# Fifteen loops over sequences, written out before, become counted loops in the engines' programs

## The chip, the cores and the metric

The kernel runs on one core of a Trainium2 chip. The metric is the device time of one execution in microseconds (us). Each of the core's five engines runs a program of its own: TensorE (PE in the profile, and PEld for its weight loads), VectorE (DVE), ScalarE (ACT), GpSimd (POOL) and SyncE (SP, which here only issues DMAs). The engines meet through semaphores alone: an instruction adds to one when it ends, another instruction waits until one has reached a number.

## The reference

The input is x, 4 sequences of 1024 tokens by 256 features. It is normalised, and the result is x plus two branches:

```
xn = layernorm(x)
out = x + attention(xn) + ffn(xn)
attention: rms norm, q/k/v for 16 heads of 64, window of 64, softmax, gate by sigmoid, W_out
ffn:       2 layers, each: shift tokens; q/k/v for 8 heads of 64; l2 norm and rotary; window of 128,
           softmax, wo, add; shift, layernorm, w1 (682 x 2), a * gelu(g), w2, add
```

All is float32. Products of activations and weights are formed as three products of a high and a low part, to keep float32's accuracy.

## The kernel before

The kernel has two phases, one after the other. `attention_phase` (L170) goes over 4 sequences and splits, on the way, the layers' weights into high and low parts. `layers_phase` (L903) goes over 8 sequences: the 4 of layer 0 and then the 4 of layer 1. A sequence is handled as two halves of 512 tokens.

What is done for a sequence stands in a table of steps, `A_ORDER` (L133) for the attention and `ORDER` (L888), taken twice, for the layers: ("scores", 0), ("softmax", 0), ("weigh", 0) and so on. In each engine's program a function `iteration(it, steps, ...)` walks through the same table and emits this engine's part of each step: TensorE the products of a "scores" (L613, L1358), VectorE the masking and the row maximum (L840, L1608), ScalarE the exponentials (L748, L1517), GpSimd the scaling of "weigh" (L522, L1236), TensorE the "transpose" (L621, L1366) and the "values" (L636, L1381). In the layers there follow the products `up` (L1406), ScalarE's Gelu of them (L1533, which needs another table than the exponentials, so that an ACT_TABLE_LOAD stands ahead of it), and `down` (L1420). The order of each engine is the order of the table.

The numbers that are waited for come from the class `Count`. One count says how many times a semaphore is raised in one iteration, and `upto` works out the value:

```
if it is None:
    return self.credit + self.unit * (n + 1)
return it * (self.unit * self.each) + (self.credit + self.unit * (self.before + n + 1))
```

Here `it` is the number of the sequence. Where it is a number of Python, the value is a constant in the instruction. The last iteration of a phase leaves out the steps that prepare a next sequence (`last`), and stands apart, as does iteration 3 of the layers for SP, PE and ACT, in which weights or tables of the other layer are loaded.

Every engine has such loops over `it`: one of 3 in the attention; in the layers one of 3 (4 for DVE and POOL) and one of 3. In the kernel before they are loops of Python: the program of an engine holds each iteration's instructions one after another.

An instruction of a compute engine holds one wait of its own. A wait before that becomes an EVENT_SEMAPHORE, an instruction of the engine's sequencer, which stands still at it. Where two waits stand before an instruction, the build decides which of the two goes into it.

TensorE's results go to three banks in turn; `take_bank` (L532, L1270) waits until the one who reads the bank of three results ago is through (semaphores `emptied` and `copied`), and the step itself waits for its operand: the transposes L621 and L1366 for `normalized`, which GpSimd raises.

## Time and profile before

| | |
|---|---|
| device time, median of 3 runs | 2094.42 us (2092.75 to 2094.42) |
| device time of the profiled execution | 2094.42 us |
| its span, first to last instruction | 2092.4 us |
| granted TensorE clock, mean | 0.978 of full speed |
| busy PE, PEld, DVE, ACT, POOL | 91%, 75%, 63%, 67%, 46% |
| records of PE, PEld, DVE, ACT, POOL | 15184, 15184, 4117, 3933, 1311 |
| one sequence of the attention | 164.6 us |
| one sequence of the layers | 164.0 us (layer 0), 166.4 us (layer 1) |

### The profile page before, as it was taken

Reading aid. Unit: us, or ns where it says so; the run is one execution under the profiler, and the core shown is the slowest. Engines: PE = TensorE matmul, PEld = TensorE weight load, DVE = VectorE, ACT = ScalarE, POOL = GpSimd, SP = SyncE. Lnnn points to the kernel's source line nnn. Section 1 sums busy time; section 2 is a strip of 40 time slices with the busy share of each in tenths; the row PEclk is TensorE's granted clock in tenths of the full one; section 3 lists DMA queues with packets and bytes.
Section 4 is the critical chain, followed back from the end, with each engine's and each line's share of the span. In section 5 each row is a group of like instructions: output and inputs, shape, how many; then the busy total and the mean of one; then the engine's idle time right before and its main releaser. Section 6 shows DMA issues by size and latency. Waiting matters only on the chain.

```text
span 2092.4 us, 42526 instructions
## 1 busy us (share of the span) xinstructions
PE 1901.2 (91%) x15184; PEld 1576.9 (75%) x15184; DVE 1322.5 (63%) x4117; ACT 1402.3 (67%) x3933; POOL 963.3 (46%) x1311
## 2 busy tenths in 40 slices
PE   5999999999998479999999999996999999999998
PEld 3777787777777358788787787885878878778777
DVE  4543543444443168778777777785777877777765
ACT  4886977878778155856757757665576675675764
POOL 1532442433334055626536547353473663654732
PEclk9999999999999689999999999998999999999999
DMA  3231231322212600110110101304011011010110
GB/s 124 90 95 46 91 105 53 95 69 90 91 51 78 228 31 11 44 44 11 41 36 22 41 11 44 104 6 149 21 44 54 21 44 54 11 52 21 34 33 26
DMA packets 120580, 121.16 MB, mean 58 GB/s; under 512 B 27172, under 2 KB 100916, under 8 KB 120372
## 3 DMA queue, kind: packets, MB, share of 16 engines
q1 hardware_dynamic: 108848, 100.89, 15.1%
q10 hardware_dynamic: 11524, 17.57, 2.4%
q8 instruction: 122, 2.00, 0.4%
q14 instruction: 86, 0.70, 0.1%
HBM read 72.78 MB, written 37.25 MB: 53 GB/s over the span
## 4 chain that ended last, share of the span: by engine, by line
PE 32%; DVE 19%; ACT 9%; POOL 3%; issue 2%; ACTq 2%; DVEq 0%; POOLq 0%
PE f_bank L1283 12%; PE f_scores L1420 4%; PE f_scores L1358 4%; ACT f_prob L1517 4%; DVE f_u L1673 4%; PE f_bank L1366 4%; PE f_bank L1406 4%; DVE f_gu L1670 2%; PE f_o_bank L1381 2%; ACT f_u L1537 2%; PE f_bank L1330 2%; DVE f_x_tok L1656 2%; DVE f_x_tok L1662 1%; POOL f_prob L1236 1%; DVE f_rstd L1649 1%
## 5 line engine op out<-in xcount | busy, mean ns | idle before, releaser
L1236 POOL TENSOR_SCALAR f_prob<-f_prob,f_row_inv 128x256 f32<-128x256 f32 x512 | 264.0, 535 | 343.7 <-DVE f_row_inv L1616 343.7
L522 POOL TENSOR_SCALAR a_prob<-a_prob,a_row_inv,a_gate 128x128 f32<-128x128 f32 x512 | 226.2, 462 | 409.7 <-DVE a_row_inv L849 409.7
L1283 PE MATMUL f_bank<-f_wqkv,f_actT 128*128 128x512 f32 x1152 | 302.8, 407 | 14.9 <-DVE f_actT L1559 14.9
L1406 PE MATMUL f_bank<-f_hT,f_w 128*128 128x256 f32 x2112 | 275.3, 285 | 7.7 <-DVE f_gu L1670 7.7
L1406 PEld LDWEIGHTS f_bank<-f_hT,f_w 128*128 128x128 f32 x2112 | 261.0, 189 | 14.3 <-DVE f_gu L1670 10.8
L1283 PEld LDWEIGHTS f_bank<-f_wqkv,f_actT 128*128 128x128 f32 x1152 | 209.1, 191 | 64.1 <-issue 17.8
L1517 ACT ACTIVATE f_prob<-f_scores,f_neg_max 128x256 f32<-128x256 f32 x512 | 236.3, 489 | 30.2 <-DVE f_neg_max L1608 29.3
L1212 POOL TENSOR_TENSOR f_norm<-f_norm,f_minus_half 128x16 f32<-128x16 f32 x64 | 199.6, 3119 | 47.1 <-DVE f_norm L1568 45.3
L1608 DVE CUSTOM_DVE_ANT_0 f_scores<-f_scores,f_mask 128x256 f32<-128x256 f32 x512 | 199.8, 455 | 15.5 <-PE f_scores L1358 15.4
L1537 ACT ACTIVATE f_u<-f_gu 128x256 fp32r<-128x256 f32 x192 | 80.2, 418 | 181.8 <-DVE f_gu L1670 181.8
L748 ACT ACTIVATE a_prob<-a_scores,a_neg_max 128x128 f32<-128x128 f32 x512 | 179.9, 391 | 29.0 <-DVE a_neg_max L840 28.7
L545 PE MATMUL a_bank<-a_xT,a_wqkv 128*128 128x512 f32 x768 | 192.7, 403 | 0.0
L1218 POOL TENSOR_TENSOR f_qk_tok<-f_qk_tok,f_tables 128x512 f32<-128x512 f32 x128 | 161.6, 1284 | 62.0 <-DVE f_sin_part L1576 62.0
L1673 DVE TENSOR_TENSOR f_u<-f_gu,f_u 128x256 fp32r<-128x256 f32 x192 | 125.7, 654 | 92.9 <-ACT f_u L1537 92.9
L1461 ACT ACTIVATE f_probT<-f_bank 128x512 f32<-128x512 f32 x256 | 146.0, 613 | 55.6 <-PE f_bank L1366 54.3
L1358 PE MATMUL f_scores<-f_kT,f_q 64*128 64x256 f32 x1024 | 149.5, 409 | 32.7 <-ACT f_prob L1517 32.1
L1366 PE MATMUL f_bank<-f_ident,f_prob 128*128 128x128 f32 x1024 | 148.7, 283 | 30.4 <-POOL f_prob L1236 17.5
L545 PEld LDWEIGHTS a_bank<-a_xT,a_wqkv 128*128 128x128 f32 x768 | 143.7, 191 | 36.0 <-issue 2.5
L1420 PE MATMUL f_scores<-f_w,f_u 128*128 128x256 f32 (+1 forms) x1152 | 163.9, 286 | 0.0
L1366 PEld LDWEIGHTS f_bank<-f_ident,f_prob 128*128 128x128 f32 x1024 | 111.6, 143 | 66.2 <-issue 37.9
L1420 PEld LDWEIGHTS f_scores<-f_w,f_u 128*128 128x128 f32 (+1 forms) x1152 | 147.7, 188 | 6.1 <-issue 2.5
L840 DVE CUSTOM_DVE_ANT_0 a_scores<-a_scores,a_mask 128x128 f32<-128x128 f32 x512 | 129.8, 325 | 35.5 <-PE a_scores L613 35.5
(124 smaller groups left out, 3847.3 us busy)
## 6 DMA issues: line engine op xcount, KB each, us to landing
split_weights<-a_hi_lo SPq DMA_DIRECT2D x16, 512.0 KB, 2.8
f_x_next<-states SPq DMA_DIRECT2D x32, 256.0 KB, 3.1
f_tables<-scaled_tables SPq DMA_DIRECT2D x16, 512.0 KB, 6.1
f_x<-states SPq DMA_DIRECT2D x16, 512.0 KB, 5.0
split_weights<-a_hi_lo SPq DMA_DIRECT2D x12, 682.0 KB, 4.1
f_w<-split_weights ACTq DMA_DIRECT2D x4, 1280.0 KB, 13.2
a_x_tok<-in_x SPq DMA_DIRECT2D x8, 512.0 KB, 4.7
states<-a_x_tok SPq DMA_DIRECT2D x8, 512.0 KB, 3.1
```

The source lines that it names most:

```text
L522: last = nc.gpsimd.tensor_scalar(part, part, row_inv[:, a % 2, head, t:t + 1], gate[:, half, t, h:h + 1], ALU.mult, ALU.mult)
L545: last = nc.tensor.matmul(out, lhs(c, a), rhs(c, b), start=(i == 0), stop=(i == len(order) - 1))
L1212: nc.gpsimd.tensor_tensor(n, n, minus_half[:], ALU.pow).then_inc(norm_ready.sem, 1)
L1236: last = nc.gpsimd.tensor_scalar(part, part, row_inv[:, a % 2, head, t:t + 1], 1.0, ALU.mult, ALU.mult)
L1283: last = nc.tensor.matmul(out, lhs(c, a), rhs(c, b), start=(i == 0), stop=(i == len(order) - 1))
L1358: mm = nc.tensor.matmul(scores[a % 2][head][:, t, :], q[rows, pair, col:col + P], kT[rows, pair, col:col + 2 * P], start=True, stop=True)
L1366: last = nc.tensor.transpose(out[:, j * P:(j + 1) * P], prob[:, a % 2, head, j // 2, (j % 2) * P:(j % 2 + 1) * P], ident[:])
L1406: mm = nc.tensor.matmul(out[:, which * PART:(which + 1) * PART], w1[:, wp, c, col:col + P], hT[:, hp, c, columns_of(a // FH)], start=(i == ...
L1420: mm = nc.tensor.matmul(y_banks[a // FH % PARTS][:, t, :], u[0:m, a % (2 * TILES), up, t * P:(t + 1) * P], w2[0:m, wp, j, :], start=(j == ...
L1517: last = nc.scalar.activation(prob[:, a % 2, head, t, :], scores[a % 2][head][:, t, :], ACT.Exp, bias=neg_max[:, a % 2, head, t:t + 1], sc ...
L1608: last = nc.vector.tensor_tensor_reduce(out=sc, in0=sc, in1=mask[:, min(half * TILES + tile + t, 1)], scale=-1.0, scalar=3e38, op0=ALU.add ...
L1673: nc.vector.tensor_tensor(u[0:m, a % (2 * TILES), LO, :], gu[0:m, a % 2, :], u[0:m, a % (2 * TILES), HI, :].bitcast(F32), ALU.subtract).th ...
```

## The change

The fifteen `for it in range(...)` loops become counted loops of the engine (`Fori`), with the same bounds. The loops' bodies, the tables of steps, tiles, transfers and the iterations that stand apart stay as they are. The diff is the same edit in ten places; the attention's five engines have one loop each, the layers' two:

```diff
@@ attention: SP L469, POOL L526, PE L662, ACT L764, DVE L878
-            for it in range(0, BATCH - 1):
+            with pe.Fori(0, BATCH - 1) as it:
                 iteration(it, steps)
             iteration(BATCH - 1, last)
@@ layers: SP L1190, PE L1425, ACT L1539 (the last with two loads between)
-            for it in range(0, BATCH - 1):
+            with pe.Fori(0, BATCH - 1) as it:
                 iteration(it, steps, 0, 0)
             iteration(BATCH - 1, steps, 0, 1)
-            for it in range(BATCH, SEQUENCES - 1):
+            with pe.Fori(BATCH, SEQUENCES - 1) as it:
                 iteration(it, steps, 1, 1)
             iteration(SEQUENCES - 1, last, 1, 1)
@@ layers: POOL L1262, DVE L1681
-            for it in range(0, BATCH):
+            with dve.Fori(0, BATCH) as it:
                 iteration(it, steps, 0)
-            for it in range(BATCH, SEQUENCES - 1):
+            with dve.Fori(BATCH, SEQUENCES - 1) as it:
                 iteration(it, steps, 1)
             iteration(SEQUENCES - 1, last, 1)
```

`it` is now a register. The value that an instruction waits for is worked out by register instructions ahead of it, and at the end of a body stand an addition and a branch back.

At TensorE, in the layers, before, where sequence 0 ends and sequence 1 begins (L1420 is `down`, L1358 "scores", L1290 the transposes of the next tokens):

```order
L1420 MATMUL f_scores<-f_w,f_u 128x256 [waits f_u_ready]
L1420 MATMUL f_scores<-f_w,f_u 128x256 x5
L1358 MATMUL f_scores<-f_kT,f_q 128x256 [waits f_exped,f_copied]
L1358 MATMUL f_scores<-f_kT,f_q 128x256 x3
L1358 MATMUL f_scores<-f_kT,f_q 128x256 [waits f_exped,f_x2_ready]
L1358 MATMUL f_scores<-f_kT,f_q 128x256 x3
L1290 MATMUL f_bank<-f_ident,f_x_next 128x128 [waits f_copied,f_emptied,f_x_loaded]
```

The same place of the changed kernel, first the end of the body:

```order
L1414 REGISTER_ALU
L1420 MATMUL f_scores<-f_w,f_u 128x256 [waits f_u_ready]
L1420 MATMUL f_scores<-f_w,f_u 128x256 x5
L1425 REGISTER_ALU
L1425 COMPARE_AND_BRANCH
```

and then its beginning, to which that branch goes (ISA is an instruction that works out several registers at once):

```order
L1425 ISA
L1353 ISA [waits f_copied]
L1358 MATMUL f_scores<-f_kT,f_q 128x256 [waits f_exped]
L1358 MATMUL f_scores<-f_kT,f_q 128x256 x3
L1351 ISA
L1358 MATMUL f_scores<-f_kT,f_q 128x256 [waits f_exped,f_x2_ready]
L1358 MATMUL f_scores<-f_kT,f_q 128x256 x3
```

A register addition and a branch have come in between `down` and "scores", and behind the branch two instructions that work out registers. Elsewhere in the body a REGISTER_ALU stands ahead of nearly every instruction that waits.

At TensorE, in the same sequence, before, the transposes of the probabilities (L1366):

```order
L1358 MATMUL f_scores<-f_kT,f_q 128x256 [waits f_exped]
L1358 MATMUL f_scores<-f_kT,f_q 128x256 x3
L1366 MATMUL f_bank<-f_ident,f_prob 128x128 [waits f_normalized,f_emptied]
L1366 MATMUL f_bank<-f_ident,f_prob 128x128 x3
L1366 MATMUL f_bank<-f_ident,f_prob 128x128 [waits f_normalized,f_copied]
L1366 MATMUL f_bank<-f_ident,f_prob 128x128 x3
```

The same in the changed kernel's body (an earlier pair of them):

```order
L1366 MATMUL f_bank<-f_ident,f_prob 128x128 x3
L1273 REGISTER_ALU
L1364 REGISTER_ALU [waits f_emptied]
L1366 MATMUL f_bank<-f_ident,f_prob 128x128 [waits f_normalized]
L1366 MATMUL f_bank<-f_ident,f_prob 128x128 x3
L1353 REGISTER_ALU
```

The waits of two-wait instructions have changed places. The names in the first of these fences are those of all waits ahead of a row; in the program a semaphore instruction holds `normalized` and the transpose holds `emptied` or `copied`. In the changed kernel the register instruction holds `emptied` and the transpose holds `normalized`.

At ScalarE, in the layers, before, where the Gelu of a sequence's first half begins:

```order
L1461 ACTIVATE f_v<-f_bank 128x512 [waits f_filled]
L1467 ACTIVATE f_hT<-f_bank 128x2x256 [waits f_filled]
L1533 ACT_TABLE_LOAD [waits f_filled]
L1533 ACTIVATE f_gu<-f_bank,f_rows 128x256 [waits f_rows_loaded]
L1537 ACTIVATE f_u<-f_gu 128x256 [waits f_emptied]
```

and in the changed kernel's body:

```order
L1466 REGISTER_ALU
L1467 ACTIVATE f_hT<-f_bank 128x2x256 [waits f_filled]
L1529 REGISTER_ALU [waits f_rows_loaded]
L1533 ACT_TABLE_LOAD
L1533 ACTIVATE f_gu<-f_bank,f_rows 128x256 [waits f_filled]
L1536 REGISTER_ALU
L1537 ACTIVATE f_u<-f_gu 128x256 [waits f_emptied]
```

`filled` is raised when TensorE has finished the first `up`. The table was loaded behind that wait, and is now loaded ahead of it. Where the Gelu of the second half begins it is the other way round. Before:

```order
L1461 ACTIVATE f_v<-f_bank 128x512 [waits f_filled]
L1467 ACTIVATE f_hT<-f_bank 128x2x256 [waits f_filled]
L1533 ACT_TABLE_LOAD [waits f_u_ready]
L1533 ACTIVATE f_gu<-f_bank,f_rows 128x256 [waits f_filled]
L1537 ACTIVATE f_u<-f_gu 128x256 [waits f_emptied]
```

and in the changed kernel's body:

```order
L1467 ACTIVATE f_hT<-f_bank 128x2x256 [waits f_filled]
L1529 REGISTER_ALU
L1531 REGISTER_ALU [waits f_filled]
L1533 ACT_TABLE_LOAD
L1533 ACTIVATE f_gu<-f_bank,f_rows 128x256 [waits f_u_ready]
L1536 REGISTER_ALU
L1537 ACTIVATE f_u<-f_gu 128x256 [waits f_emptied]
```

Here the table load stood behind a wait for an `up` of the first half and ahead of `filled`, and stands now behind `filled`.

## Rows read from the trace of the kernel before

**Rows 1.** The page, busy time of each engine

```profile
PE 1901.2 (91%) x15184; PEld 1576.9 (75%) x15184; DVE 1322.5 (63%) x4117; ACT 1402.3 (67%) x3933; POOL 963.3 (46%) x1311
```

**Rows 2.** Stretches: us, busy (x) of PE, PEld, DVE, ACT, POOL, PEclk, DMA, GB/s

```profile
207.10:371.70 164.60, 156.75 (x1449) 126.85 (x1448) 74.15 (x371) 128.63 (x413) 62.99 (x134) 0.99 0.25 80
1090.20:1254.20 164.00, 156.42 (x1178) 131.90 (x1177) 125.71 (x328) 109.78 (x285) 85.99 (x94) 1.00 0.10 32
```

**Rows 3.** The page, DMA queues of the programs: packets, MB, share of 16 engines

```profile
q8 instruction: 122, 2.00, 0.4%
q14 instruction: 86, 0.70, 0.1%
```

**Rows 4.** Timeline of PE, an attention sequence's first instructions: start us, us, instruction

```profile
207.14 1.98 PE L613 MATMUL a_scores<-a_kT,a_q 64*64 64x128 f32 x64
```

**Rows 5.** L605 in 204 to 208 us: ns min/median/max, first and last start

```profile
L605 PEldq EVENT_SEMAPHORE  x2: 51/51/51, 205.2 to 207.4; - x2
```

**Rows 6.** Timeline of all engines, end of a layer sequence

```profile
1087.99 2.46 PE L1420 MATMUL f_scores<-f_w,f_u 128*128 128x256 f32 x17
1090.18 0.48 PE L1358 MATMUL f_scores<-f_kT,f_q 64*128 64x256 f32 x1
1091.64 0.43 DVE L1608 CUSTOM_DVE_ANT_0 f_scores<-f_scores,f_mask 128x256 f32<-128x256 f32 x1 [0.34 <-PE f_scores L1358]
1092.55 0.47 ACT L1517 ACTIVATE f_prob<-f_scores,f_neg_max 128x256 f32<-128x256 f32 x1 [1.85 <-DVE f_neg_max L1608]
```

**Rows 7.** L1353 and L1677 in 1080 to 1092 us

```profile
L1353 PEldq EVENT_SEMAPHORE  x2: 51/51/51, 1088.8 to 1089.5; - x2
L1677 DVEq EVENT_SEMAPHORE  x2: 21/21/21, 1088.3 to 1088.4; - x2
```

**Rows 8.** DMA issues: KB each, median us from issue to landing

```profile
f_x_tok<-f_x SPq DMA_DIRECT2D x16, 0.5 KB, 1.7
f_x_tok<-f_x SPq DMA_DIRECT2D x32, 15.0 KB, 2.2
a_kT<-a_k_kept SPq DMA_DIRECT2D x32, 32.0 KB, 2.8
```

**Rows 9.** Sequencer instructions of two lines, whole span

```profile
L1364 PEldq EVENT_SEMAPHORE  x256: 51/51/51, 768.2 to 2049.8; - x128
L907 SPq COMPARE_BRANCH  x1: 33/33/33, 2091.7 to 2091.7; - x1
```

**Rows 10.** Timeline at 235.5 to 236.1 us, a wait held by the sequencer

```profile
235.33 0.46 POOL L522 TENSOR_SCALAR a_prob<-a_prob,a_row_inv,a_gate 128x128 f32<-128x128 f32 x1
235.93 0.41 PE L621 MATMUL a_bank<-a_ident,a_prob 128*128 128x128 f32 x2 [0.92 <-POOL a_prob L522]
```

**Rows 11.** Timeline at 974.0 to 974.4 us, a wait held by the instruction

```profile
973.77 0.48 DVE L1662 SCALAR_TENSOR_TENSOR f_x_tok<-f_x_tok,f_rstd,f_rows 128x256 f32<-128x256 f32 x1
974.30 0.33 PE L1299 MATMUL f_bank<-f_ident,f_x_tok 128*128 128x128 f32 x1 [0.24 <-DVE f_x_tok L1662]
```

**Rows 12.** Waits: us in total, times, longest

```profile
PE f_bank L1366 <- POOL f_prob L1236: 17.5, 45, 0.7
PE f_bank L1366 <- DVE f_actT L1559: 11.3, 14, 0.8
PE a_bank L621 <- POOL a_prob L522: 10.0, 13, 1.1
PE a_bank L621 <- ACT a_v L697: 8.3, 8, 1.8
PE f_bank L1299 <- DVE f_x_tok L1662: 7.1, 16, 4.0
```

**Rows 13.** Timeline of ACT, first Gelu of a first half, then of a second

```profile
815.49 1.28 ACT L1533 ACT_TABLE_LOAD   x1 [3.93 <-PE f_bank L1406]
816.79 0.48 ACT L1533 ACTIVATE f_gu<-f_bank,f_rows 128x256 f32<-128x256 f32 x1
897.47 0.47 ACT L1533 ACTIVATE f_gu<-f_bank,f_rows 128x256 f32<-128x256 f32 x1 [2.58 <-PE f_bank L1406]
```

More of the change, by code:

```diff
@@ L467, in iteration @@
                         sp.dma_start(rows_out[it // HALVES], rows[:]).then_inc(rows_stored.sem, 16)
-            for it in range(0, BATCH - 1):
+            with sp.Fori(0, BATCH - 1) as it:
                 iteration(it, steps)
@@ L524, in iteration @@
                             last.then_inc(normalized.sem, 1)
-            for it in range(0, BATCH - 1):
+            with pool.Fori(0, BATCH - 1) as it:
                 iteration(it, steps)
@@ L660, in iteration @@
                         gates_back(it, a)
-            for it in range(0, BATCH - 1):
+            with pe.Fori(0, BATCH - 1) as it:
                 iteration(it, steps)
@@ L762, in iteration @@
                         nc.scalar.activation(hi_lo[:, HI, 0:width(a)], raw[:, 0:width(a)], ACT.Copy).then_inc(weights_hi.sem, 1)
-            for it in range(0, BATCH - 1):
+            with act.Fori(0, BATCH - 1) as it:
                 iteration(it, steps)
@@ L876, in iteration @@
                                                 ALU.subtract).then_inc(weights_split.sem, 1)
-            for it in range(0, BATCH - 1):
+            with dve.Fori(0, BATCH - 1) as it:
                 iteration(it, steps)
@@ L1188, in iteration @@
                         sp.dma_start(place[:, two, :], x1[:, two, :]).then_inc(x2_stored.sem, 16)
-            for it in range(0, BATCH - 1):
+            with sp.Fori(0, BATCH - 1) as it:
                 iteration(it, steps, 0, 0)
             iteration(BATCH - 1, steps, 0, 1)
-            for it in range(BATCH, SEQUENCES - 1):
+            with sp.Fori(BATCH, SEQUENCES - 1) as it:
                 iteration(it, steps, 1, 1)
@@ L1260, in iteration @@
                             pool.sem_inc(attended_added.sem, 1)
-            for it in range(0, BATCH):
+            with pool.Fori(0, BATCH) as it:
                 iteration(it, steps, 0)
-            for it in range(BATCH, SEQUENCES - 1):
+            with pool.Fori(BATCH, SEQUENCES - 1) as it:
                 iteration(it, steps, 1)
@@ L1423, in iteration @@
                         mm.then_inc(downed.sem, 1)
-            for it in range(0, BATCH - 1):
+            with pe.Fori(0, BATCH - 1) as it:
                 iteration(it, steps, 0, 0)
             iteration(BATCH - 1, steps, 0, 1)
-            for it in range(BATCH, SEQUENCES - 1):
+            with pe.Fori(BATCH, SEQUENCES - 1) as it:
                 iteration(it, steps, 1, 1)
@@ L1537, in iteration @@
                         nc.scalar.activation(u[0:m, a % (2 * TILES), HI, :], gu[0:m, a % 2, :], ACT.Copy).then_inc(u_hi.sem, 1)
-            for it in range(0, BATCH - 1):
+            with act.Fori(0, BATCH - 1) as it:
                 iteration(it, steps, 0, 0)
@@ L1544, in _ @@
             load_others(1)
-            for it in range(BATCH, SEQUENCES - 1):
+            with act.Fori(BATCH, SEQUENCES - 1) as it:
                 iteration(it, steps, 1, 1)
@@ L1679, in iteration @@
                         nc.vector.tensor_tensor(x1[:, two, :], y_banks[a % PARTS][:], x1[:, two, :], ALU.add).then_inc(x2_ready.sem, 1)
-            for it in range(0, BATCH):
+            with dve.Fori(0, BATCH) as it:
                 iteration(it, steps, 0)
-            for it in range(BATCH, SEQUENCES - 1):
+            with dve.Fori(BATCH, SEQUENCES - 1) as it:
                 iteration(it, steps, 1)
```

## The prediction

> **What bounds the kernel now.** I read the page's busy times first, then the busy times of one sequence of each phase, then the order around the places where a loop will branch back, and last the queues through which the programs come in. TensorE is busy 91% of the span [rows 1]. One attention sequence takes 164.60 us, of which PE is busy 156.75, at a granted clock of 0.99; one layer sequence takes 164.00 us with 156.42 [rows 2]. So PE idles some 8 us in a sequence, and an instruction of PE that comes late delays the rest unless it eats one of these short waits. No other engine comes near: the next is ACT with 128.63. What matters is therefore (a) whether PE's instruction stream stops where a loop branches back, (b) whether the added register instructions slow the stream down, (c) what the exchanged waits do.
>
> The profiled execution took 2094.42 us, span 2092.4 and 2.0 around it; 2094.42 is also the median of the runs, so the sum starts there.
>
> **Fetching the programs: what it costs now.** Queue q8 brings 122 packets, 2.00 MB, thus 16.4 KB each [rows 3]. PE has 15184 products and 15184 weight loads [rows 1], with its semaphore instructions about 31,400; over 122 packets that is 256 instructions a packet and 64 bytes an instruction. The whole program passes once, one packet per 2092/122 = 17 us. Loops cannot win here what isn't lost now: the shares of 0.4% and 0.1% [rows 3] are no load. A packet's own time is 0.4% of 16 x 2092.4 us, over 122, = 1.1 us. The same for the other engines' queue, q14: 0.70 MB in 86 is 8.1 KB each, 0.1% x 16 x 2092.4 / 86 = 0.4 us.
>
> **The branch back.** A body of the changed PE program has 3096 instructions in the attention (the 1449 + 1448 of [rows 2] and the rest semaphores and registers), 2534 in the layers: 12.1 and 9.9 packets of 256. PE branches back twice in the attention (3 turns) and twice in each of the two layer loops: 6 times, near 207, 372, 926, 1090, 1601 and 1768 us. Now each packet comes while older ones are worked on. Behind a branch the beginning of the body, ten packets old, has to come again if the engine keeps only a few, and nothing can be executed until it has. I take that it does: a queue that carries each instruction exactly once shows prefetch in order and nothing of a store for whole bodies.
>
> The stall: no row shows one. The nearest is a DMA's time from issue to landing [rows 8]: 1.7 us for 0.5 KB, 2.2 for 15 KB, 2.8 for 32 KB. A packet has 16.4 KB, so 2.2, and I add its own 1.1 us, since it goes through one ring as one packet where the others are spread: 3.3. Low end 1.7 + 1.1 = 2.8, high end 2.8 + 1.1 = 3.9. With the addition, the branch and two register instructions (4 x 51 ns at most, [rows 9]) 3.5 us from the branch to the next product.
>
> What covers it is how far PE's sequencer runs ahead of the array. In the attention the semaphore instruction of the next "scores" is executed at 205.2 [rows 5] and its product L613 starts at 207.14 [rows 4]: a lead of 1.94 us. Cost 3.5 - 1.94 = 1.56, twice: 3.1. In the layers L1353's is at 1088.8 [rows 7], L1358 starts at 1090.18 [rows 6]: lead 1.38, cost 2.12, four times: 8.5. Behind L1358 stand the mask on DVE at 1091.64 and the exponentials at 1092.55 [rows 6], so the delay is handed on. Together 11.6 us. With the low end of the stall (3.0 in all) it is 1.06 x 2 + 1.62 x 4 = 8.6, with the high one (4.1) 2.16 x 2 + 2.72 x 4 = 15.2; with a packet that lands within the lead, 0.
>
> The Trainium skill (Runtime: NRT & Kernel Launch, Instruction fetch mechanics) says that prefetch is purely sequential and that a taken branch out of the two blocks at hand forces a fetch of its target before execution goes on. The rows of q8 agree on the sequence and the block's size; the stall itself no row of before shows. By that rule the sum is the one above.
>
> The other engines branch too, at the same places and on DVE and POOL once more, at 1254. DVE's last wait instruction of the body is executed at 1088.4 [rows 7]; its instructions would be there again by 1088.4 + 2.2 + 0.4 + 0.1 = 1091.1, before the mask at 1091.64 [rows 6]. ACT has until 1092.55. I cost these at nothing; the cover on DVE is 0.5 us thick and PE's own lateness thickens it to 2.6. If it is gone, some 0.5 to 1 us a branch.
>
> **The register instructions.** In all of the execution PE gets 1245 REGISTER_ALU and 60 ISA more and 351 EVENT_SEMAPHOREs fewer, 954 in balance; ACT 1500, DVE 956, POOL 342, SP 414. A sequencer instruction takes 21 ns (DVE) to 51 ns (PE) in the rows [rows 7, 9]. All exposed, PE's would be 954 x 0.051 = 49 us, the upper bound; the lower is 0. PE's sequencer runs 1.4 to 1.9 us ahead at the two places read, and a register instruction is executed while the array works through four or more products, two of which take 0.41 us [rows 10]; where PE waits, the addition is done ahead of the wait. I take 1 us, near the lower bound, since an EVENT_SEMAPHORE of 51 ns ahead of a running array costs nothing today [rows 9].
>
> **The exchanged waits.** A wait that the sequencer holds costs more after its release than one inside the instruction: POOL ends at 235.79, the transpose starts 235.93, 0.14 us [rows 10]; DVE ends at 974.25, L1299 starts at 974.30, 0.05 [rows 11]. So 0.09 us a wait. Transposes L1366 waited 45 times for POOL and L621 13 times [rows 12]; six of eight layer sequences and three of four attention ones are in loops, so 44 waits x 0.09 = 3.9 us won. It is lost where the second semaphore is the late one: L1366 for DVE 14, L1299 for DVE 16, L621 for ACT 8 [rows 12], 28 in loops, 2.6 us. Net -1.3, I take -1. Bounds: -3.9 and +2.6.
>
> **The Gelu's table.** The first load today begins behind `filled`, takes 1.28 us, and the Gelu follows at 816.79; in the second half the Gelu is released by `up` itself at 897.47, its load done before [rows 13]. The change exchanges the two: 1.28 x 6 = -7.7 in the first halves, +7.7 in the second. Both Gelus stand on the same way to `down`, so I take 0. One of them alone deciding gives -7.7 or +7.7.
>
> **Sum.** 2094.4 + 11.6 + 1 - 1 + 0 = 2106 us.
>
> **The rivals.**
>
> *A: the branch is hidden or cheap.* Either the engine has the beginning at hand, or the packet lands within PE's lead of 1.4 to 1.9 us. For it: all is fetched ahead today, and the small DMA's 1.7 us lies between the two leads. Then six branches of 0.1 us and the exchanges: 2093 to 2097. Against it: a body is ten packets. The Trainium skill (Advanced Engine Details and Errata, Control Flow Timing) gives a compare-and-branch about 108 ns; that alone would make 0.65 us of six. No trace here shows a branch on PE.
>
> *B: longer stalls.* The beginning of a body in the layers lies 0.69 into a packet of 256, so the next packet is wanted 79 instructions on; if it comes only behind the first, 1.1 us more, six times, 6.6; and if DVE's or ACT's branch ends last, another 0.5 to 1 each. 11.6 + 6.6 + 1 gives 2114 to 2120, and with a high end of the stall 2125. For it: two fetches start together; against it: 79 instructions on PE are 7 or more us of array work in which to get one packet, unless the array has run empty.
>
> *C: registers on the path.* ACT gets 1500 instructions and PE 954; if a fifth to a half of PE's 49 us is exposed, 10 to 25 us over the stalls: 2116 to 2135. Against it stands PE's lead.
>
> *D: faster.* No stall (A), and the table loads one-sided: a first half's Gelu 1.28 us sooner feeds `down`, while the second half's load, later, lies under PE's other work. It decides if PE idles for the first half's `down` and not for the second's. -7.7 + 0.6 - 1: 2087. For it is the exposed 3.93 us ahead of the first load [rows 13]; against it the second half's Gelu waits as well, 2.58 us, and A must hold too.
>
> **How the numbers follow.** Forecast (2100 to 2112) 0.51; A 0.14; B 0.21; C 0.09; D 0.05. A measurement of this kernel tells a change of about 0.2%, 4.2 us, from none, so no change is 2090.2 to 2098.6: A, 0.14. Faster is D, 0.05. Slower are the rest, 0.81. The range runs from 2096, which takes in A's upper part and the low end of the stall with a one-sided table gain, to 2124, which takes in B; outside lie D, half of A and half of C, about 0.17.
>
> **What the profile of the changed kernel would show.** Right: q8 carries about as many packets as before and, at each of PE's six branches, one or two out of turn, beginning when the sequencer branches; PE idle 1.5 to 2.2 us more ahead of the first L613 and L1358 of a sequence at these six, and not where an iteration stands apart; sequences otherwise of 164 us to within 0.5; the transposes' waits for POOL shorter by 0.1 each; the Gelu's load before `filled` in the first half. Wrong: no packet at a branch (A), a second idle time some 79 instructions behind it or one of DVE or ACT (B), bodies longer by over 2 us with the idle time spread evenly over PE (C), or layer sequences below 163 us (D).

## The result: slower by 1.44%, and the profile after

The changed kernel takes 2123.99 us (median of 4, 2119.74 to 2127.86) against 2093.86 of the kernel before on the same chip: ratio 1.0144, 95% interval 1.0124 to 1.0165. The prediction's direction was right and its size was not: +11.6 were forecast, +30 came, and its range ended at 2124, 0.01 above the median, which is luck and no merit of the sum. The profiled execution took 2126.16 us, 1.8 of it around its span of 2124.4; so 32.0 us of span have to be found.

The page of the changed kernel, against [rows 1, 3]:

```profile
PE 1918.1 (90%) x15184; PEld 1585.8 (75%) x15184; DVE 1329.3 (63%) x4117; ACT 1404.3 (66%) x3934; POOL 963.6 (45%) x1311
q8 instruction: 137, 2.24, 0.5%
q14 instruction: 128, 1.05, 0.2%
```

No engine has more instructions of work, but PE is busy 16.9 us longer for the same 15184 products. That was in no term of the prediction, and it is the first hint at the clock. q8 brings 15 packets more. TensorE executes 954 instructions more, 4 packets; the other 11 fall on 6 branches, about two to each.

The branches of PE, one row a loop of three turns (least, median, most ns; the least is the last turn, which isn't branched back):

```profile
L662 PEldq COMPARE_BRANCH  x3: 83/3312/3343, 204.8 to 543.1; - x3
L1425 PEldq COMPARE_BRANCH  x3: 83/3860/3887, 934.4 to 1273.9; - x3
L1428 PEldq COMPARE_BRANCH  x3: 82/3472/4000, 1624.7 to 1964.9; - x3
```

A branch not taken takes 0.08 us, one taken back 3.3 to 4.0: the stall of the prediction (3.3, bounds 2.8 and 3.9) stands in the record itself. In the trace's packets of q8 it has three parts at each of the six: 0.9 to 1.1 us from the branch's start to the packet's, 0.9 to 1.5 us for the packet, and 1.4 to 1.5 us until the next instruction is executed. The timeline of PE at such a place in the attention, and then in layer 0:

```profile
208.50 0.89 PE L613 MATMUL a_scores<-a_kT,a_q 64*64 64x128 f32 x24 [1.75 <-issue]
212.81 2.41 PE L613 MATMUL a_scores<-a_kT,a_q 64*64 64x128 f32 x40 [3.42 <-issue]
```

```profile
1108.31 1.34 PE L1358 MATMUL f_scores<-f_kT,f_q 64*128 64x256 f32 x9 [2.45 <-issue]
1111.51 2.07 PE L1358 MATMUL f_scores<-f_kT,f_q 64*128 64x256 f32 x7 [1.85 <-issue]
```

"issue" says that nothing in the profile was waited for: the instruction wasn't there. It is so twice, the second time in the middle of a row of equal products. And the products behind it are slow: 7 take 2.07 us, where 9 took 1.34. The stretches of the attention's place, with the columns of [rows 2]:

```profile
208.20:209.40 1.20, 0.89 (x24) 0.73 (x25) 0.00 (x0) 0.00 (x0) 0.00 (x0) 1.00 0.99 329
209.40:212.80 3.40, 0.00 (x0) 0.00 (x0) 0.00 (x0) 0.00 (x0) 0.00 (x0) 0.91 0.93 277
212.80:219.00 6.20, 6.19 (x49) 5.09 (x49) 4.26 (x34) 4.14 (x25) 0.95 (x3) 0.50 0.06 16
219.00:222.00 3.00, 3.00 (x37) 2.28 (x40) 0.36 (x2) 3.00 (x14) 3.00 (x8) 1.00 0.00 0
208.50:378.08 169.58, 158.58 (x1445) 127.63 (x1445) 74.52 (x371) 128.52 (x413) 62.96 (x134) 0.98 0.26 79
1108.30:1278.06 169.76, 162.18 (x1198) 135.91 (x1199) 126.60 (x328) 110.24 (x284) 86.03 (x94) 0.98 0.10 31
```

Behind the second stall the granted clock is 0.50 for 6.2 us (1.2 GHz instead of 2.4). In the kernel before it is low at this place too, behind the 1.81 us wait ahead of L621, but for a shorter time (0.66 on the mean of 217 to 222, and 1.00 from there). A sequence takes 169.6 and 169.8 us instead of 164.6 and 164.0 [rows 2].

At the boundary that only VectorE and GpSimd branch at, VectorE alone is late:

```profile
1275.64 0.69 DVE L1679 TENSOR_TENSOR f_x<-f_scores,f_x 128x512 f32<-128x512 f32 x1 [1.26 <-PE f_scores L1420]
1278.84 0.43 DVE L1608 CUSTOM_DVE_ANT_0 f_scores<-f_scores,f_mask 128x256 f32<-128x256 f32 x1 [2.51 <-issue]
```

```profile
L1681 DVEq COMPARE_BRANCH  x1: 68/68/68, 1275.7 to 1275.7; - x1
L1681 DVEq FUSED_REGOPS  x1: 63/63/63, 1278.6 to 1278.6; - x1
```

VectorE's branch record is short (0.07 us), and the stall is the 2.9 us until its next record. In the kernel before VectorE idled 0.34 us ahead of the mask [rows 6].

Each instruction of PE compared with the same one in the kernel before gives this, in us later (worked out from the two traces). "Settled" is how much the lateness has grown from just ahead of the boundary to 30 us and more behind it. In the layers the very first product of a body is 0.2 us later than the one given:

| place in the kernel before | first product | second stall adds | settled, over the boundary |
|---|---|---|---|
| 207, 372 (attention) | 1.8, 1.9 | 3.6, 3.5 | 5.0, 4.3 |
| 926, 1090 (layer 0) | 2.6, 2.6 | 2.0, 2.2 | 5.1, 5.1 |
| 1254 (VectorE) | | | 2.7 |
| 1601, 1768 (layer 1) | 2.2, 2.8 | | 3.1, 3.5 |
| sum | 13.9 | 11.3 | 28.8 |

The seven boundaries hold 28.8 of the 32.0 us. "Settled" is less than the two stalls and the clock together in the attention, since waits behind them (the 1.81 us ahead of L621 at 216.36) shrink, and since the kernel before has a stretch of half clock there itself. One execution differs from another in its half clock: between the boundaries the profiled executions of the kernels below lie from 1.6 us under the kernel before to 6.7 over it, and the one with short pauses, which has no register instructions, is 4.8 over it.

### The profile page after: what moved, and what is told of

Same layout as the page of the kernel before. It is cut to its first block, busy times and chain, and to the rows that moved or that the text cites. A ratio compares the mean times of both kernels' runs of the same rounds, so it can differ in the third digit from the quotient of the medians.

```text
span 2124.4 us, 46932 instructions
## 1 busy us (share of the span) xinstructions
PE 1918.1 (90%) x15184; PEld 1585.8 (75%) x15184; DVE 1329.3 (63%) x4117; ACT 1404.3 (66%) x3934; POOL 963.6 (45%) x1311
## 4 chain that ended last, share of the span: by engine, by line
PE 29%; DVE 14%; issue 10%; ACT 8%; POOL 3%; ACTq 2%; DVEq 0%; POOLq 0%
PE f_bank L1283 10%; PE f_scores L1420 4%; PE f_scores L1358 4%; ACT f_prob L1517 4%; PE f_bank L1406 4%; PE f_bank L1366 3%; DVE f_gu L1670 3%; PE f_bank L1330 2%; DVE f_x_tok L1656 2%; PE f_o_bank L1381 2%; ACT f_u L1537 2%; DVE f_x_tok L1662 1%; DVE f_sin_part L1576 1%; DVE f_rstd L1649 1%; POOL f_prob L1236 1%
## 5 line engine op out<-in xcount | busy, mean ns | idle before, releaser
L1406 PEld LDWEIGHTS f_bank<-f_hT,f_w 128*128 128x128 f32 x2112 | 261.0, 189 | 14.0 <-DVE f_gu L1670 10.4
L1358 PE MATMUL f_scores<-f_kT,f_q 64*128 64x256 f32 x1024 | 157.8, 428 | 44.2 <-ACT f_prob L1517 30.7
L1366 PE MATMUL f_bank<-f_ident,f_prob 128*128 128x128 f32 x1024 | 151.3, 285 | 26.5 <-DVE f_actT L1559 9.9
L1420 PE MATMUL f_scores<-f_w,f_u 128*128 128x256 f32 (+1 forms) x1152 | 163.8, 286 | 0.0
L1366 PEld LDWEIGHTS f_bank<-f_ident,f_prob 128*128 128x128 f32 x1024 | 112.1, 143 | 65.2 <-issue 33.7
L1358 PEld LDWEIGHTS f_scores<-f_kT,f_q 64*128 64x128 f32 x1024 | 98.1, 200 | 81.6 <-ACT f_prob L1517 39.4
```

What stands on the lines that cost most here:

```text
L1358: mm = nc.tensor.matmul(scores[a % 2][head][:, t, :], q[rows, pair, col:col + P], kT[rows, pair, col:col + 2 * P], start=True, stop=True)
L1366: last = nc.tensor.transpose(out[:, j * P:(j + 1) * P], prob[:, a % 2, head, j // 2, (j % 2) * P:(j % 2 + 1) * P], ident[:])
L1406: mm = nc.tensor.matmul(out[:, which * PART:(which + 1) * PART], w1[:, wp, c, col:col + P], hT[:, hp, c, columns_of(a // FH)], start=(i == ...
L1420: mm = nc.tensor.matmul(y_banks[a // FH % PARTS][:, t, :], u[0:m, a % (2 * TILES), up, t * P:(t + 1) * P], w2[0:m, wp, j, :], start=(j == ...
```

## The experiments

Theory T: the time lies at the boundaries, as a branch's stall less its cover, a second fetch behind it, VectorE's branch, and the half clock after each. Rivals: the other engines' branches (R1), the register instructions and exchanged waits (R2). The changed kernel's own values stand above. Before is 2093.8 to 2094.9 in all groups.

**TensorE alone, and all but TensorE.** For all but TensorE, the edit in the changed kernel, at TensorE's loop of the attention and likewise at its two of the layers:

```diff
-            with pe.Fori(0, BATCH - 1) as it:
+            for it in range(0, BATCH - 1):
                 iteration(it, steps)
```

For TensorE alone the same three lines change the other way round, in the kernel before.

> Only TensorE's three loops are counted; the other engines hold each iteration written out, as before. Theory T (from the two traces): the added time lies where TensorE branches back. Its branch record lasts 3.3 to 4.0 us at each of the six places, in four of them a second stall of 2 to 3.6 us follows (the body's beginning lies near the end of a fetched block of 256 instructions, and the next block is asked for only then), and the granted clock is half for some microseconds behind. By T nearly all of the 32 us stay but the 2.65 us at 1254, where only VectorE and GpSimd branch: 2094 + 29 = 2123 (2119 to 2125). Rival R1, the other engines' branches end last and TensorE's is mostly hidden: 2094 to 2110. Rival R2, register instructions on all engines carry it: TensorE has 954 of 4166, so under 2105.

Measured: 2126.64, ratio 1.0155 (1.0138 to 1.0172). TensorE's loops alone cost as much as all; R1 and R2 fall as main causes. The time lies above T's range (2119 to 2125), and not 2.7 us below the changed kernel's. In the trace the boundary at 1254 costs nothing, as expected, but the attention's two cost 6.1 each instead of 5.0 and 4.3: the granted clock was 0.50 in 213 to 217 and still 0.72 in 217 to 223.

> All engines but TensorE have counted loops. VectorE's branch stands behind its last L1679, which begins at 1090.61 (1254.68 for the next sequence), and the record after its branch came 2.9 to 3.2 us later in the changed kernel; the mask was due at 1091.64 (1255.71). So T, where VectorE counts once TensorE no longer is late: 2.0 us late at each of five places in the layers, with the clock's part 2.65 as measured at 1254, and up to 2 at two places in the attention: 2094 + 5 x 2.65 + 2 to 4 = 2109 to 2112. If only TensorE's branches mattered and 1254 were an exception: 2097. R1, the others carry all: 2115 to 2124.

Measured: 2117.07, 1.0110 (1.0093 to 1.0127). T's figure was too low, and the time lies in R1's range: T took the 2.65 us at 1254 for the price of each, and here, settled, the boundaries of the layers cost 2.5 to 3.8 (3.8 at 1254: 2.2 by VectorE's lateness, the rest behind it, where the granted clock is 0.59 in 1272 to 1279) and the attention's 3.3 and 3.2, where T had up to 2. 32.7 and 23.2 us can't be added: they fill the same gaps, since in the changed kernel VectorE's branch stands 1.8 to 2.1 us behind TensorE's and is through 0.8 to 1.9 us after it.

**VectorE alone, and SyncE, ScalarE and GpSimd.** Only the loops of the engines named are counted.

> Counted loops on VectorE alone. Theory T: the 23 us of the kernel with all but TensorE counted are VectorE's: 2115 to 2118. Rival: the engines add up there (SyncE's loads or ScalarE's branch late too): 2104 to 2112.

Measured: 2116.65, 1.0099 (1.0084 to 1.0113). VectorE's waits "issue" in this kernel:

```profile
DVE f_scores L1608 <- issue: 12.5, 5, 2.8
DVE a_scores L840 <- issue: 8.8, 4, 3.1
```

That is 2.5 us at each of five places in the layers, and in the attention four waits at two places: VectorE too has a second stall there, in the middle of a row of equal instructions:

```profile
209.57 0.30 DVE L840 CUSTOM_DVE_ANT_0 a_scores<-a_scores,a_mask 128x128 f32<-128x128 f32 x1 [2.96 <-issue]
213.86 0.30 DVE L840 CUSTOM_DVE_ANT_0 a_scores<-a_scores,a_mask 128x128 f32<-128x128 f32 x1 [1.44 <-issue]
```

These are idle times of VectorE. What TensorE loses by them, settled, is 3.1 us at each of the attention's two places and 2.3 to 4.0 at the layers' five, together the 23 us.

> Counted loops on SyncE, ScalarE and GpSimd alone. Theory T: ScalarE's next record comes 2.6 us after its branch, 6 us before its exponentials are due in the attention and during the wait ahead of them in the layers, GpSimd idles there, SyncE's loads are early: all hidden, 2092 to 2098. Then the 23 us of the kernel with all but TensorE in counted loops are VectorE's. Rival: those three carry a part of the 23 us: 2100 to 2117.

Measured: 2095.04, 1.0006 (0.9996 to 1.0016). In this kernel three of the five engines loop at no price.

**Where the body begins in a fetched block.** The edit, 64 and then 96 times (here and below the line that makes the semaphore is left out):

```diff
+            for _ in range(64):
+                pe.sem_inc(pe_padded, 1)
             pe.wait_ge(consts_loaded, 16 * CONSTS)
             transpose_x(None, HALVES - 1)
```

> The changed kernel with 64 semaphore instructions more on TensorE at its very start, where it idles 17 us: nothing else changes but where the bodies begin within the fetched blocks of 256 instructions. Left in the first block behind the branch are some 55 instructions (attention), 22 (layer 0) and 173 (layer 1) in the changed kernel; with the pad 247, 214 and 109. T: the second stall goes in the attention (3.6 us, twice) and in layer 0 (2.2 us, twice), and none comes in layer 1, since 109 instructions there last longer than the 3.4 us that a block takes: 2124 - 11.6 = 2112 (2109 to 2116), below if the clock recovers sooner. If the second stall is something else (DMA traffic at the loop's start, a wait), nothing changes: 2122 to 2126.

Measured: 2116.18, 1.0101 (1.0084 to 1.0118), 8 us below the changed kernel and just above T's range (2109 to 2116); the profiled execution, from which the lines are, was the longest, 2123.09. The attention's second stall is gone:

```profile
PE a_scores L616 <- issue: 4.1, 2, 2.1
L665 PEldq COMPARE_BRANCH  x3: 83/3609/3613, 204.6 to 537.9; - x3
L1428 PEldq COMPARE_BRANCH  x3: 83/5027/5031, 930.5 to 1268.7; - x3
```

(L665 and L1428 are the attention's and layer 0's loops here.) Two waits of at most 2.1 us, where the changed kernel has `PE a_scores L613 <- issue: 10.3, 4, 3.4`. Layer 0's second stall is gone too, but its branch takes 5.03: in the trace the packet of the next block in order starts at 931.22 and that of the branch at 931.52, and they take 1.9 and 1.8 us side by side.

> The changed kernel with 96 semaphore instructions at TensorE's start. With 64 of them the second stall was gone in the attention, but layer 0's branches took 5.03 us instead of 3.6 to 3.9: there the branch stands 16 instructions behind the beginning of a block, the next block in order has just been asked for, and two blocks travelled at once (1.8 to 1.9 us each instead of 1.0). With 96 the branches stand 65, 48 and 153 instructions into a block, and behind them are left 215, 182 and 77. Theory T (place within the block decides): all six branches 3.3 to 4.0 us, no second stall, some 2.5 us a seam: 6 x 2.5 + 2.7 to 4 at 1254 = 2112 to 2114. Rival (5.03 us belongs to layer 0's traffic and not to the place): 2116 again, with branches of 5 us.

Measured: 2118.28, 1.0124 (1.0106 to 1.0142). The mechanism was as T said: the branch of layer 0 is back at 3.5, and four waits at four places in the layers mean that no second stall is left:

```profile
PE f_scores L1361 <- issue: 7.8, 4, 2.5
L1428 PEldq COMPARE_BRANCH  x3: 83/3484/3522, 929.2 to 1263.4; - x3
L1431 PEldq COMPARE_BRANCH  x3: 83/3364/3802, 1617.1 to 1958.1; - x3
```

The time was not: 2112 to 2114 were expected. Settled, the attention's boundaries cost 2.4 and 2.5, layer 0's 2.4 each, layer 1's 2.4 and 3.7 and the one at 1254 3.9, 19.7 us in all and little more than T's 17.7 to 19. The other 4.5 us of this execution lie between the boundaries, and T's sum had nothing for them. Part of both is the clock. The same 16 products behind a branch of layer 0 and one of layer 1:

```profile
932.97 2.00 PE L1361 MATMUL f_scores<-f_kT,f_q 64*128 64x256 f32 x16 [2.06 <-issue]
1620.75 3.68 PE L1361 MATMUL f_scores<-f_kT,f_q 64*128 64x256 f32 x16 [1.23 <-issue]
```

The clock falls behind some stalls and not behind others (1.00 in 932 to 935, 0.64 in 1620 to 1623), and not behind the longer one here. It also falls where no stall is near: it was 0.67 in 1612 to 1615, ahead of the branch at 1617.1, which cost 1.5 us.

> The changed kernel with 96 semaphore instructions at TensorE's start (2118), and VectorE's loops written out as before. Theory T: the seam at 1254, 4.0 us in that run, is VectorE's alone and goes; at the six others TensorE ends last, with VectorE's branch 1.9 us behind it and back 0.6 us after it, so that up to 0.6 us goes at each: 2118 - 4.0 - 0 to 3.6 = 2110 to 2114. Rival (the others' branches at 1254 count): 2117 to 2119.

Measured: 2112.27, 1.0080 (1.0064 to 1.0095), as T said; at 1254 nothing is left.

**The stall without a fetch.** The kernel before, with this in each of TensorE's loops (68, then 23, ahead of the second and third turn):

```diff
             for it in range(0, BATCH - 1):
+                for _ in range(68 if it > 0 else 0):
+                    pe.sem_inc(a_paused, 1)
                 iteration(it, steps)
```

> The kernel before, its loops written out, with nothing fetched out of turn; TensorE's program has 68 semaphore instructions of 51 ns (3.47 us) at the six places where the changed kernel branches back. Theory T (a late sequencer, and the half clock that follows TensorE's idling, are all there is to the first stall): as much as a seam of the padded kernel without a second stall, 2.5 us, of which about 1.6 to 2.1 are the stall less its cover and the rest the clock: 2094 + 15 = 2109 (2105 to 2111), and the granted clock falls to half for 2 to 5 us behind each pause. Rival (the price comes from the fetch itself, its traffic or the engines' branches together): the clock stays at full and the time is under 2103.

Measured: 2154.61, 1.0291 (1.0274 to 1.0308). The pause was mis-sized: the instructions' records last 51 ns, but they follow one another by 153. With 10.4 us the first products are 8.5 (attention) and 9.1 to 9.2 us late, which is 10.4 less the leads of 1.94 and 1.38: the cover of the prediction, to 0.2 us.

> The pauses again, with 23 semaphore instructions each: in the run with 68 they followed one another by 153 ns, not by the 51 ns of their records, so that a pause was 10.4 us. 23 x 0.153 = 3.5 us, the length of the branch's stall. Theory T: 3.5 less the lead (1.9 and 1.4) = 1.6 twice and 2.1 four times = 11.6, and up to 1 to 1.6 us of half clock at each: 2106 to 2112. Rival (the price is the fetch's): under 2100.

Measured: 2108.17, 1.0061 (1.0046 to 1.0076). +13 to 14 us with nothing fetched out of turn, within T's range; the profiled execution has 11.3 of it at the six places, settled. The first product is 1.65 to 1.7 us late in the attention and 2.0 to 2.2 in the layers, by the prediction's 1.56 and 2.12:

```profile
1098.57 2.00 PE L1362 MATMUL f_scores<-f_kT,f_q 64*128 64x256 f32 x16 [2.01 <-issue]
```

T's half clock came at some of the pauses only: behind both of layer 0, of which this is one, the granted clock stayed at 1.00. So a late sequencer alone carries most of what a first stall costs, 11.3 us here against 15.8 at the same six places of the kernel padded with 96.

**Where the branch stands.** The edit at TensorE in the attention (in the layers at ("scores", 2); VectorE at the same step in the attention and at ("weigh", 3) in the layers; and the padding of above, 100 and 40, so that no second stall comes in either):

```diff
-            with pe.Fori(0, BATCH - 1) as it:
-                iteration(it, steps)
-            iteration(BATCH - 1, last)
+            first, rest = cut_at(steps, ("transpose", 0))
+            iteration(0, first)
+            with pe.Fori(0, BATCH - 1) as it:
+                iteration(it, rest)
+                iteration(it + 1, first)
+            iteration(BATCH - 1, cut_at(last, ("transpose", 0))[1])
```

> All loops counted as in the changed kernel, but TensorE's and VectorE's bodies begin elsewhere in the table of steps, as many branches as before are taken back. TensorE branches ahead of ('transpose', 0) in the attention, where it waited 1.81 us in the kernel before (L621 at 216.36), and ahead of ('scores', 2) in the layers, where it waited 1.02 (L1358 at 1094.54); VectorE ahead of its part of ('scores', 3) in the attention (wait 2.04 at 219.64) and of ('weigh', 3) in the layers (wait 2.48 at 1103.69). 100 semaphore instructions at TensorE's start and 40 ahead of the layers place the beginnings 22, 170 and 21 instructions into a block, the branches 47, 146 and 253. Theory T (the stall of 3.5 us costs what cover does not hide: TensorE's lead of 1.4 to 1.9 us and the wait that stood there): attention 3.5 - 1.9 - 1.8 = 0, layers 3.5 - 1.4 - 1.0 = 1.1 four times, VectorE 3.0 - 2.5 = 0.5 five times and 3.0 - 2.0 = 1.0 twice where it ends last: 2094 + 4.4 + 2 to 4.5 = 2100 to 2104. Rival (a seam costs about the same wherever it stands, since all engines wait for TensorE): 2116 to 2124.

Measured: 2107.39, 1.0059 (1.0045 to 1.0073). With as many branches taken the loss is 12 to 13 us, against 24 in the kernel padded with 96 and 30 in the changed one. It is more than T gave (2100 to 2104). T's layers came at or below its 1.1 us a boundary (0 to 1.1), its attention didn't, 2.5 and 2.7 instead of 0: the branch took 3.9 us there. VectorE's waits "issue" are of at most 0.3 us.

```profile
212.42 1.10 PE L621 MATMUL a_scores<-a_kT,a_q 64*64 64x128 f32 x32
217.03 1.32 PE L629 MATMUL a_bank<-a_ident,a_prob 128*128 128x128 f32 x5 [3.51 <-POOL a_prob L528]
...
L672 PEldq COMPARE_BRANCH  x3: 83/3918/3962, 212.8 to 546.7; - x3
```

The array had worked off what lay ahead of the branch by 213.5 (212.42 + 1.10), 0.7 us behind the branch's start at 212.8; a lead of 1.9 us was read at another place and doesn't hold at this one.

**How long a body may be.** Ahead of the kernel before, at TensorE (at VectorE alike, with the sizes below):

```diff
+            for size in (32, 200, 400, 600, 1000, 1800):
+                with pe.Fori(0, 3) as turn:
+                    for _ in range(size):
+                        pe.sem_inc(pe_turned, 1)
```

> The kernel before with loops of semaphore instructions put ahead of its work, whose time is not of interest: on TensorE bodies of 32, 200, 400, 600, 1000 and 1800 instructions, on VectorE of 16, 100, 200, 300 and 500, three turns each. Read is the time from the branch to the next instruction. Theory T1, only the block that is executed and the next stay at hand (two blocks of 256, on VectorE of 128): about 0.1 us up to 200 instructions on TensorE (100 on VectorE), 3.3 to 4 us from 600 (300) on, 400 (200) by its place. Rival T2, eight blocks stay at hand on TensorE (128 KB): 0.1 us up to 1800, 3.3 us only in the kernel's bodies of 2534 and 3096. Rival T3, every taken branch fetches: 3.3 us for 32 too.

TensorE's loops of 600, 1000 and 1800 instructions, by the order of time:

```profile
L584 PEldq COMPARE_BRANCH  x3: 76/208/223, 386.7 to 570.9; - x3
L584 PEldq COMPARE_BRANCH  x3: 76/208/217, 724.8 to 1031.3; - x3
L584 PEldq COMPARE_BRANCH  x3: 79/3727/3803, 1308.0 to 1869.0; - x3
```

> Bodies of 1100 to 1600 instructions in steps of 100 on TensorE and of 340, 380, 420 and 460 on VectorE, ahead of the kernel before. In the run with six sizes the branch was 0.21 us up to 1000 on TensorE and 3.8 at 1800, on VectorE 0.3 us to the next instruction up to 300 and 2.8 to 2.9 at 500. If eight blocks of 256 are held on TensorE of which some are for what comes next, the step lies at one whole number of blocks: 1280 or 1536 (by where the body begins, 256 less); on VectorE, four blocks of 128, at 384 less the body's offset.

All eighteen branches of TensorE's six loops:

```profile
L584 PEldq COMPARE_BRANCH  x18: 76/208/232, 170.0 to 3726.7; - x18
```

No branch over 0.24 us up to 1600 instructions: on TensorE the beginning of a body is kept up to 1600 and is gone at 1800. On VectorE it was 0.2 to 0.3 us to the next instruction up to 300 and 2.7 to 2.9 from 340 on. So none of the three holds as given: on TensorE T1 fails at 600 instructions, T3 at 32 and T2 at 1800. On TensorE neither of the steps that were named for the run between fits; on VectorE three blocks of 128 less the body's offset can. The kernel's bodies, 2534 and 3096 on TensorE and some 475 on VectorE, are beyond both. The Trainium skill (Advanced Engine Details and Errata, ISA Cache) gives TensorE 128 KB and two cache lines of 256 instructions: two lines of 256 don't fit these rows (1600 instructions are over six), and 128 KB, 2048 instructions of 64 bytes, lies above what was kept.

**The register instructions and the exchanges.** At TensorE in the attention, and alike in every loop of every engine:

```diff
-            for it in range(0, BATCH - 1):
-                iteration(it, steps)
+            for turn in range(0, BATCH - 1):
+                with pe.Fori(turn, turn + 1) as it:
+                    iteration(it, steps)
```

> Each of the iterations stands in a counted loop of its own of one turn, on all engines: all the register instructions and the exchanged waits of the changed kernel are there, no branch is taken back, and every instruction is again fetched in order once. T: between the branches the changed kernel's TensorE drifts by less than 1 us a sequence against the kernel before (-0.4 in a first half, +1.0 in a second half of the layers, -0.5 in the attention), so 2094 + 0 to 4 = 2094 to 2098. R2 (register instructions on the path): 2105 to 2124.

Measured: 2093.96, 1.0001 (0.9991 to 1.0011). This run doesn't test what it was meant to: the build worked out `it` itself, and TensorE executed 9 register additions, not 1245. It shows that branches not taken cost nothing. So the number was made a register that the build can't know (TensorE in the attention; the other loops of the four compute engines alike):

```diff
-            for it in range(0, BATCH - 1):
-                iteration(it, steps)
+            counted = pe.alloc_register("a_counted")
+            pe.reg_mov(counted, 0)
+            with pe.Fori(0, 2) as turn:
+                pe.reg_add(counted, counted, 1)
+            pe.reg_alu(counted, counted, 1, ALU.bitwise_and)
+            base = pe.snap(counted, min_val=0, max_val=1)
+            for turn in range(0, BATCH - 1):
+                iteration(base + turn, steps)
```

> TensorE, VectorE, ScalarE and GpSimd hold each iteration written out, but its number is a register (worked out at run time by a loop of two short turns) plus a constant, so that their programs execute the register instructions of the changed kernel (TensorE 1238 additions, ScalarE 1664, VectorE 930, GpSimd 290) with the same exchanged waits and table loads, and no long loop branches back. SyncE's loops are plain. Theory T: between the seams the changed kernel's TensorE falls behind by 3 us in all: 2094 to 2098. Rival R2, register instructions on the path: 2100 to 2115.

Measured: 2096.3, 1.0007 (0.9998 to 1.0015): 1.5 us with an interval from -0.4 to 3.1. R2 falls.

The exchanges alone, in the kernel before; first the table's:

```diff
-                        if a == 0:
-                            act.wait_ge(rows_loaded, loads(1, layer))
                         act.wait_ge(filled.sem, filled.upto(it, n))
+                        if a == 0:
+                            act.wait_ge(rows_loaded, loads(1, layer))
```

> Only ScalarE's pair of waits ahead of the first Gelu is swapped, the rest is the kernel before. T: the Gelu comes 1.28 us sooner behind the first `up`, of which 0.35 us a sequence reaches TensorE: 2094 - 2.8 = 2091 (2090 to 2093). If all of it did: 2094 - 10 = 2084. If none: 2094.

Measured: 2090.27, 0.9978 (0.9969 to 0.9987): 4.6 us faster than the kernel before (by the interval 2.7 to 6.5). The first Gelu comes at `up`'s end, with no load ahead of it, against [rows 13]:

```profile
813.58 0.48 ACT L1533 ACTIVATE f_gu<-f_bank,f_rows 128x256 f32<-128x256 f32 x1 [2.58 <-PE f_bank L1406]
```

In the trace TensorE gains 0.4 to 0.5 us on the kernel before behind the first Gelu of a sequence, and 3.6 over the layers, where T had 2.8. Another 1.9 us of this execution lie in the attention, where nothing was changed; most of that is one stretch of half clock fewer, at 217 to 221.

> The kernel before, with constants and loops written out, in which two pairs of waits stand in the other order: ScalarE waits for `filled` before the rows ahead of the first Gelu, so that the table load comes ahead of `filled`, and the transposes L621 and L1366 wait for `normalized` before they take a bank, so that the instruction holds `normalized`. The prediction's terms for these: 0.09 us at each of 58 waits, 5.2, less up to 3.5 where the bank is late; a first half of the layers in the changed kernel ran 0.35 us shorter, eight of them 2.8. T: 2094 - 2.8 - 1.7 = 2089 to 2092. Rival, it is absorbed by the next wait: 2092 to 2096.

With, besides, `normalized` waited for ahead of the bank at L621 and L1366. Measured: 2092.33, 0.9986 (0.9977 to 0.9994). The table's gain is there (3.7 us over the layers in the trace), and the exchanged waits of the transposes add nothing to it. The 2 us between the two medians aren't settled by the intervals.

## Why the prediction was wrong

- *One execution of each PE packet, in order; a branch back fetches.* Right. 3.3 to 4.0 us a branch, forecast 3.3, with 2.8 and 3.9 as ends. That the size fits is partly luck: the sum had 2.2 us for a DMA and 1.1 for the packet, and of the three measured parts the longest at five of the six branches is the 1.4 to 1.5 us behind the packet, for which it had no term of its own.
- *PE's cover, 1.94 and 1.38 us.* Right at both places, shown by the pauses. The first products were 1.8 to 2.8 us late, 13.9 in sum, forecast 11.6. The Trainium skill's rule on taken branches (Runtime: NRT & Kernel Launch, Instruction fetch mechanics) holds for these bodies; its window of two pages doesn't, since bodies of 1600 instructions on TensorE, over six of its packets, and of 300 on VectorE, over two of its packets of 8.1 KB, were not fetched again.
- *"79 instructions on PE are 7 or more us of array work in which to get one packet."* This step failed, by which rival B was set aside. The bodies begin later in their block than I had counted (22 instructions were left in layer 0, not 79, and some 55 in the attention), the instructions are short there (24 products in 0.89 us), and the second packet's instructions come only 3.4 to 4.6 us after the first's. For the attention the kernel before showed it: with 64 products of "scores" in 1.98 us [rows 4], 79 instructions, some 40 products and their weight loads, are 1.2 us of array work and not 7. B priced the stall at 1.1 us; it cost 2.0 to 3.6 at four places, 11.3 in sum, and padding took it away (2124 to 2116, though layer 0's branches grew by 1.1 there). Both signs named for B appeared, a second idle time and VectorE's. That 2124 lies near B's high end (2125) is luck too, since B had nothing for the clock.
- *No term for the clock.* The prediction counted PE's products at one speed. Behind a stall the granted clock was 0.50 for up to 6.2 us; PE is busy 16.9 us more. Part of it meets waits. This is the second missing piece, and the one that can't be sized in advance from these runs: of two like stalls one has it and one hasn't, and the kernel padded with 96 has it once without a stall. How much of the 28.8 us is the clock's was not separated, and what decides was not tried.
- *"DVE's last wait instruction of the body is executed at 1088.4."* The step failed. The branch does not stand behind the last wait instruction but behind the last L1679, which starts at 1090.61 since it waits for PE. From there 2.9 us make 1093.5, 1.9 behind the mask's 1091.64, not 0.6 ahead of it. It cost 2.7 at 1254, and where PE is written out 23 us in all, a second stall of VectorE in the attention among them.
- *ACT, POOL and SP hidden.* Right (2095).
- *Register instructions, 1 us; exchanges -1; the table 0.* Right together: 2096.3, +1.5. But the table's zero was a difference of two terms: the early load in the first halves alone is worth 4.6 us by the medians (3.6 in the trace's layers), and the changed kernel gives it back in the second halves: in its six counted sequences of the layers TensorE gains 0.4 to 0.5 us behind the first Gelu and loses 0.4 to 0.5 behind that of the second half, which the kernel with TensorE alone counted doesn't.
- The sum by the measured sizes, settled: 28.8 at seven boundaries, and 3.2 between them. The kernel of the register instructions has 3.2 too in its profiled execution, but by its median only 1.5, so that part of it may be the one execution's clock.

## What to carry to other kernels

A loop over a long body is paid where it branches back: look up how many instructions its engine's body has, how late in the body's last work the branch is reached, and what stands right behind it. On the engine that waits or is waited for, a body under what is kept cost 0.2 to 0.3 us a turn here, a longer one 3 to 4 us less the cover, perhaps a second fetch, and then the clock; the engines with slack looped for nothing. And where an instruction needs a table load, state its waits so that the load doesn't stand behind the one that comes last.

## What the runs showed of the hardware that I had not expected

- A taken branch out of reach stands in TensorE's record itself (3.3 to 4.0 us), on VectorE behind it (0.07 us, then 2.7 to 3.2).
- TensorE kept bodies up to 1600 instructions, not 1800; VectorE up to 300, not 340.
- VectorE has the second stall too (1.44 us in the attention, 26 instructions behind its branch).
- Behind such a branch the next block isn't yet on its way: its instructions came 3.4 (layers) to 4.6 us (attention) after the first's. In the attention they were the later ones, where DMAs keep the engines at 0.93 to 0.99; whether that is why wasn't tried.
- Branch and block begin close together (16 instructions): the branch takes 5.03 us.
- In a row of EVENT_SEMAPHOREs on TensorE records of 51 ns follow one another by 153 ns.
